# Linear attention in a decoder kernel: the inverse root of its group norm and one rotation product on GpSimd

## The reference

```python
q, k = silu(x @ Wq), silu(x @ Wk)             # 16 heads of 16 channels
# rotation of each head (halves x1, x2 of 8 channels)
concat([x1 * cos - x2 * sin, x1 * sin + x2 * cos])
scores = einsum('bthd,bshd->bhts', q, k) * D   # decay matrix, causal
o = einsum('bhts,bshd->bthd', scores, v)
x = o * sigmoid(x_in @ Wg1 @ Wg2)              # gate
ms = mean(x*x over the 16 channels of a head)
x = x * rsqrt(ms + 1e-6) * weight              # group norm
out = x @ Wo
```

## Time and profile before

| | us |
|---|---|
| median of 3 runs (lowest, highest) | 1303.86 (1300.84, 1304.48) |
| the profiled execution | 1305.45 |
| its span in the trace | 1303.5 |
| linear attention in it, first to last instruction | about 290 to 464 |

### The profile page before, as it was taken

One profiled execution on the slowest core, in us unless ns is written; L12 is line 12 of the kernel. 1 busy time (PEld: TensorE's weight loads), 2 busy tenths in 40 slices (PEclk: granted clock), 3 DMA queues, 4 the chain that ended last, 5 costly groups with the idle time before them and its releaser, 6 DMA issues. The chain is left out here.

```text
span 1303.5 us, 24606 instructions
## 1 busy us (share of the span) xinstructions
PE 1171.4 (90%) x7393; PEld 820.5 (63%) x7394; DVE 776.0 (60%) x1914; ACT 573.5 (44%) x1505; POOL 604.1 (46%) x752
## 2 busy tenths in 40 slices
PE   8996888958999689969999999999999669999995
PEld 5874555634555434457888888888888436666663
DVE  5554788856888669936676777676676322222221
ACT  3343666633333200026666666666666223233331
POOL 2002466534655447545566666566665112322232
PEclk9998999979999889979999999999999879999998
DMA  7000000004996040060000000000003113232323
GB/s 262 0 0 17 14 14 16 9 1 114 201 205 132 1 167 1 1 261 1 5 14 14 17 14 20 12 12 12 16 13 137 38 33 49 41 48 42 47 43 86
DMA packets 46372, 69.44 MB, mean 53 GB/s; under 512 B 4608, under 2 KB 42816, under 8 KB 45248
## 3 DMA queue, kind: packets, MB, share of 16 engines
q1 hardware_dynamic: 37152, 52.95, 15.2%
q0 software_dynamic: 7152, 9.34, 4.4%
q10 hardware_dynamic: 2000, 6.29, 1.3%
HBM read 57.12 MB, written 32.58 MB: 69 GB/s over the span
## 5 line engine op out<-in xcount | busy, mean ns | idle before, releaser
L1753 PE MATMUL ga.pkq<-ga.xnT,g.early 128*128 128x128 f32 x1280 | 157.1, 276 | 1.0 <-ACT ga.halves L1671 1.0
L1753 PEld LDWEIGHTS ga.pkq<-ga.xnT,g.early 128*128 128x128 f32 x1280 | 151.7, 193 | 9.6 <-issue 8.2
L1533 POOL TENSOR_TENSOR ga.halves<-ga.halves,g.ga_sinT 128x512 f32<-128x512 f32 x80 | 103.2, 1290 | 51.7 <-ACT ga.halves L1671 51.7
L1797 PE MATMUL ga.turn_out<-g.early,ga.aT 128*128 128x256 f32 x512 | 118.3, 385 | 0.3 <-ACT ga.aT L1693 0.3
L1678 ACT ACTIVATE ga.e<-ga.psc,ga.negmax 128x128 f32<-128x128 f32 x256 | 90.7, 366 | 46.8 <-DVE ga.negmax L1599 45.9
L1541 POOL TENSOR_TENSOR ga.kqT<-ga.by_cos,ga.halves 128x512 f32<-128x512 f32 x80 | 102.7, 1283 | 16.2 <-issue 16.2
L1797 PEld LDWEIGHTS ga.turn_out<-g.early,ga.aT 128*128 128x128 f32 x512 | 95.9, 192 | 12.7 <-ACT ga.aT L1693 0.7
L1908 DVE TENSOR_TENSOR ex.hidden<-ex.silu,ex.p 128x512 f32<-128x512 f32 x39 | 26.8, 687 | 124.9 <-PE ex.p L1961 118.5
L1586 DVE TENSOR_TENSOR ga.by_cos<-ga.pkq,g.ga_cosT 128x512 f32<-128x512 f32 x80 | 55.3, 691 | 72.4 <-PE ga.pkq L1753 44.5
L1778 PE MATMUL ga.paT<-ga.pT,ga.v 128*128 128x512 f32 x128 | 68.4, 616 | 12.4 <-ACT ga.pT L1686 9.2
L1885 POOL TENSOR_TENSOR ex.token<-ex.token_d,ex.zero 128x1 uint32<-128x1 uint32 x39 | 7.0, 180 | 155.0 <-DVE ex.y L1914 140.6
(11 more groups left out here) (292 smaller groups left out, 2612.1 us busy)
## 6 DMA issues: line engine op xcount, KB each, us to landing
mo_rows<-in_pad_rows SPq DMA_DIRECT2D x1, 18447.0 KB, 100.1
ex.row<-mo_rows SPq DMA_DIRECT2D x39, 129.0 KB, 2.0
g.spare<-in_mo_w SPq DMA_DIRECT2D x1, 4096.0 KB, 12.3
g.late<-in_mo_w SPq DMA_DIRECT2D x1, 4096.0 KB, 22.7
g.early<-in_mo_w SPq DMA_DIRECT2D x1, 4096.0 KB, 13.0
g.ctxT<-in_ctxR SPq DMA_DIRECT2D x1, 2048.0 KB, 13.0
xa.ctxT<-in_ctxT SPq DMA_DIRECT2D x16, 128.0 KB, 2.5
g.spare<-cv_rows SPq DMA_DIRECT2D x1, 2048.0 KB, 8.3
```

The source lines that it names most:

```text
L1533: nc.gpsimd.tensor_tensor(by_sin[:, par, :].rearrange("p (h t) -> p h t", h=REP), halves[:, par, :].rearrange("p (h t) -> p h t", h=REP), ...
L1753: last = nc.tensor.matmul(pkq[:, par, j * P:(j + 1) * P], w[:, q, at * P:(at + 1) * P], xnT[:, s.par, q, :], start=(q == 0), stop=(q == C ...
L1797: last = nc.tensor.matmul(pout, aT[:, h // REP, (h % REP) * P:(h % REP + 1) * P], g.ga_wo[:, h, :], start=(h == 0), stop=(h == H - 1))
```

## The change

In the group norm of linear attention the power on GpSimd is replaced: VectorE makes the bit estimate after the scaling of msq, and GpSimd runs scaled_rsqrt on the 128x16 tile. The factor 8/3 is divided out of the output weights in the one-time multiplication of la_wo. Of the rotation's two products, by_sin moves from VectorE to GpSimd, behind the root and ahead of the sum; by_cos stays. ScalarE's next silu waits for both.

```diff
@@ GpSimd, step
                 if a.on:
                     pool.wait_ge(msq_ready, upto(a))
-                    nc.gpsimd.tensor_tensor(norm[:], msq[:], g.minus_half[:].broadcast_to([P, H]), ALU.pow).then_inc(norm_ready, 1)
+                    scaled_rsqrt(nc, pool, norm[:], msq[:], work[:]).then_inc(norm_ready, 1)
                 if s.on:
+                    pool.wait_ge(silu_ready, upto(s))
+                    halves = qk[:].rearrange("p (h t d) -> p h t d", t=2, d=8)
+                    nc.gpsimd.tensor_tensor(by_sin[:].rearrange("p (h t d) -> p h t d", t=2, d=8), halves[:, :, ::-1, :],
+                                            spread(g.la_sin, 1, 2 * H), ALU.mult).then_inc(sin_ready, 1)
+                    pool.drain()
                     pool.wait_ge(rot_ready, upto(s))
@@ VectorE, ahead of the steps
-                last = nc.vector.tensor_scalar(g.la_wo[:, c, :], g.la_wo[:, c, :], g.la_norm[:, c:c + 1], None, ALU.mult)
+                last = nc.vector.tensor_scalar(g.la_wo[:, c, :], g.la_wo[:, c, :], g.la_norm[:, c:c + 1],
+                                                        1.0 / RSQRT_SCALE, ALU.mult, ALU.mult)
@@ VectorE, step
-                    nc.vector.tensor_scalar(msq[:], msq[:], 1.0 / HD, 4e-6, ALU.mult, ALU.add).then_inc(msq_ready, 1)
+                    nc.vector.tensor_scalar(msq[:], msq[:], 1.0 / HD, 4e-6, ALU.mult, ALU.add)
+                    dve.drain()
+                    rsqrt_seed(nc, norm[:], msq[:]).then_inc(msq_ready, 1)
@@
                     nc.vector.tensor_tensor(by_cos[:].rearrange("p (h t d) -> p h t d", t=2, d=8), halves,
-                                            spread(spread(g.la_cos, 1, 2), 1, 2 * H), ALU.mult)
-                    nc.vector.tensor_tensor(by_sin[:].rearrange("p (h t d) -> p h t d", t=2, d=8), halves[:, :, ::-1, :],
-                                            spread(g.la_sin, 1, 2 * H), ALU.mult).then_inc(rot_ready, 1)
+                                            spread(spread(g.la_cos, 1, 2), 1, 2 * H), ALU.mult).then_inc(rot_ready, 1)
@@ ScalarE, step
                     if s.past(1):
                         act.wait_ge(rot_ready, upto(s, back=1))
+                        act.wait_ge(sin_ready, upto(s, back=1))
                     nc.scalar.activation(qk[:], pqk[:], ACT.Silu).then_inc(silu_ready, 1)
```

More of the change, by code:

```diff
@@ L845, in linear_attention @@
         u, usq = m.sb("u", [P, D]), m.sb("usq", [P, D])
-        msq, norm = m.sb("msq", [P, H]), m.sb("norm", [P, H])
+        msq, norm, work = m.sb("msq", [P, H]), m.sb("norm", [P, H]), m.sb("work", [P, H])
         un, unT = m.sb("un", [P, D]), m.sb("unT", [P, C, P])
@@ L860, in linear_attention @@
         (var_ready, rstd_ready, xn_ready, turned, xnT_ready, qk_done, silu_ready, v_done, v_ready, wg_done, wg_ready,
-         gate_ready, rot_ready, qk_ready, qk_turned, kT_ready, qT_ready, scores_done, a_ready, av_done,
+         gate_ready, rot_ready, sin_ready, qk_ready, qk_turned, kT_ready, qT_ready, scores_done, a_ready, av_done,
          oT_ready, o_turned, u_ready, usq_ready, msq_ready, norm_ready, un_ready, un_turned, unT_ready, out_done,
@@ L864, in linear_attention @@
             "var_ready", "rstd_ready", "xn_ready", "turned", "xnT_ready", "qk_done", "silu_ready", "v_done", "v_ready",
-            "wg_done", "wg_ready", "gate_ready", "rot_ready", "qk_ready", "qk_turned", "kT_ready",
+            "wg_done", "wg_ready", "gate_ready", "rot_ready", "sin_ready", "qk_ready", "qk_turned", "kT_ready",
             "qT_ready", "scores_done", "a_ready", "av_done", "oT_ready", "o_turned", "u_ready", "usq_ready",
```

## The result

The changed kernel takes 1334.34 us (median of 6, 1333.4 to 1336.9) against 1303.63 for the kernel before: ratio 1.0234, 95% interval 1.0222 to 1.0246. That is 30.7 us more, where 27.9 over the median was forecast (1331.5), inside the range. The sum was close partly by luck: two of its terms were too large and one was missing, so it is worth taking apart.

A forecast was written before the change was run, and what follows sets the result against it. A dependency loop of 9.34 us per linear attention step was taken as the bound. 14 steps at 1.84 (0.83 root, 1.01 port) plus 2.0 for two last steps made 27.7 us: 1331.5 us forecast, range 1315 to 1337.

The forecast's parts named there:

- The loop, and by_sin beside it: Linear attention: a closed dependency loop of 9.34 us from un to un sets the step; by_sin is not in it.
- The root, +0.83 per step: Ten small GpSimd instructions give VectorE the norm at 4.18 us after msq's scaling; un started at 3.35 before.
- The port, +1.01: un, with two SBUF inputs, stands until GpSimd's by_sin is through, adding 1.01 us per step inside the loop.
- The sum qkr hidden: GpSimd's sum qkr, now waiting for by_sin and by_cos, still precedes TensorE's transposes, with 0.6 us of slack.
- VectorE freed gains 0: Taking by_sin's 0.68 us off VectorE only widens its idle time before the output add: gain 0.
- The clock: TensorE's granted clock was expected to stay at 1.00 despite some 2 us idle per step before un's transpose.
- the main case: Root and port both cost, 1.84 us per step, forecast 1331.5 us, own range 1324 to 1337; chance 0.68.
- The rival: TensorE's clock falls: a quarter of the steps slowed, some 4 us each, 14 us more, 1345; chance 0.07.
- the step of about 11.2: Sign in the profile after: the linear attention step of 9.34 us becomes about 11.2 us.
- the granted clock of 1.00 throughout: Sign in the profile after: TensorE's granted clock stays at 1.00.

The follow-up runs named there:

- four of ten: Changed kernel with only the first four of the root's ten GpSimd instructions (second refinement left out): 1301.79 us, ratio 0.998 to the kernel before.
- the fill: Changed kernel with by_sin's GpSimd product replaced by a fill of zeros over 1152 columns that reads nothing of SBUF: 1313.69 us, ratio 1.0075 to the kernel before.
- the reduction: Changed kernel with un as a VectorE reduction over an axis of length one, norm waited for but not applied: 1315.09 us, ratio 1.0077 to the kernel before.
- the added wait: Changed kernel with by_sin on GpSimd made to wait for un, so that VectorE reads first: 1322.80 us, ratio 1.0138 to the kernel before.
- the fill takes 5 to 6 us of that back: Changed kernel plus unread 128x512 matmuls on TensorE before the wait for un: 1328.44 us with one, 1329.2 with two.
- The kernels with one cause each: Kernel before plus only the ten-instruction root with its seed and la_wo factor: 1318.72 us; kernel before plus only by_sin on GpSimd behind the power: 1314.19 us.
- both with the clock held up: Changed kernel plus one unread 128x512 matmul on TensorE before the wait for un: 1328.44 us, ratio 1.0186 to the kernel before.

## Why the prediction was right, and where it was off

1. *The loop, and by_sin beside it*: right. With VectorE's load off and nothing else in the way (four of ten) the step stays as it was (9.39 us in the mean, 9.37 before).
2. *The root, +0.83 per step*: the sign was right, the size a little high. It measures 0.73 alone: 4.12 where 4.18 was worked out, against 3.39 in the mean of all fourteen steps before, where 3.35 was taken from two. The ten take 3.28 from first to last start where 3.38 was worked out: in the row taken the first of them lasted 0.40, here it is as short as the others (in the steps outside the loop it isn't, 0.34, and there the ten take 3.40). VectorE has the norm 0.26 after the last start, not 0.30. A quarter of the width took only 4.03 down to 3.28, since it is the spacing that counts: 0.35 to 0.38 with a drain between two, and 0.18 from the last of them to by_sin, where no drain stands.
3. *The port, +1.01*: right in kind, shown from both sides: who reads (the fill, the reduction) and who is first (the added wait). It measures 0.92, because by_sin takes 1.13 and not 1.27. It reads a small table spread over the heads, the row taken a larger one; whether that makes the difference was not tested. Of the rule as I used it, "two SBUF inputs" is not all: a tensor-scalar product is held too, an exception that the prediction left out. It did not bear on a_mat, which kept its 2.29.
4. *The sum qkr hidden*: right. It ended at 400.77, and TensorE reached the transposes at 401.62.
5. *VectorE freed gains 0*: right, see point 1.
6. *The clock*: this is the step that failed. It was priced at nothing in the main case, because cross attention kept the full clock at 8 us of 10 busy, and given 0.07 as a rival at 14 us. The clock did fall, in six of fourteen steps, some 8.7 us in the profiled execution; the fill takes 5 to 6 us of that back in the medians. The rival was off as well, the other way: it had a quarter of the steps slowed at 4 us each, and there were more of them at some 1.5. The row I took as evidence against it does have such a wait in it, but once:

```profile
131.68 0.44 PE L762 MATMUL xa.turn<-g.ident,xa.qkn 128*128 128x128 f32 x2 [1.76 <-DVE xa.qkn L615]
```

The next one there is 0.46 (at 140.81). Here a wait of 2 us came in every step. Why some steps with it ran slow and others not, no run tells. Of the signs given for the main case, the step of about 11.2 came true at the full clock (11.25), and the granted clock of 1.00 throughout did not.

So the 27.7 forecast was in truth 25 of root and port, 2.9 less than worked out, and 6 to 9 of clock, which made up for it: that the time came within 3 us of the forecast is luck, as far as these two errors cancel. The kernels with one cause each add up: 10 to 15 for the root, 10.5 for the sine, against 24 for both with the clock held up.

## What to carry to other kernels

Before work is moved between VectorE and GpSimd, find the loop that sets the step: relief outside it is worth nothing, and a wait put in it costs in every step. Then list what VectorE runs at the moment at which GpSimd will run a wide instruction. Beside one that reads SBUF, an instruction with both inputs in SBUF, or a tensor-scalar product, stood still here until GpSimd was through, while a reduction and a product out of PSUM passed. A fill let the two-input product pass and held a tensor-scalar product; the power of 128x16 let that same form pass. A chain of small GpSimd instructions with drains is priced by its count (here 0.36 us each), so ten of them lose to one power of 2.91 us at 16 columns, even though cross attention uses the same ten for 64.

## What the runs showed of the hardware that I had not expected

- A tensor-scalar product with one tensor input (128x256, 0.35 us alone) is held by a GpSimd product just as a two-input product is (1.19). In the kernel before, a product of 128x4 with a constant is held from 0.17 to 1.15, and a fill holds xn from 0.41 to 1.07, while the power of 2.91 us doesn't hold it at all (0.40).
- A stall of 2 us in each step of 11 takes TensorE's granted clock down in six of fourteen steps and makes four matmuls last 2.08 in place of 1.13. One matmul of 1 us in the gap, read by nobody, makes the whole program 5.9 us faster by the medians.
- GpSimd's product with a table spread over 32 groups and reversed halves of 8 takes 1.13 us for 128x512, less than the 1.27 of a plain sum of two tiles of that size, so the reversed order doesn't make it dear. What makes it cheaper was not tested.
